# Second attention of a two-layer AdaLN block: one written-out turn per row tile, row and column parts of the array, mask added by VectorE

## The chip, the cores and the metric

One core of a Trainium2 chip. Times are device microseconds (us) of that core; a stage of the kernel is read from the profiled execution. Engines: TensorE (PE; PEld is its weight load), VectorE (DVE), ScalarE (ACT), GpSimd (POOL), SyncE (SP).

## The reference, cut to what matters

Two layers over x of 2048 rows by 512. Layer 0: AdaLN, windowed attention, AdaLN, a mixture of experts. Layer 1: AdaLN, the attention below, AdaLN, a feed-forward network with Hadamard transforms. What the change touches is the first half of layer 1 (all float32):

```
x   = x0 + sum over 8 slots of route_w[row, j] * y_moe[pos[row, j]]    # gathered expert rows
h   = layernorm(x) * (1 + scale) + shift
q   = rope(h @ Wq + bq)                    # 16 heads of 32
k,v = rope(h @ Wk + bk), h @ Wv + bv       # 4 key heads of 32, each serves 4 query heads
s   = q k^T / sqrt(32), masked: a row sees the 16 first keys (meta) and the last 128, never later ones
x   = x + gate * (softmax(s) v @ Wo + bo)
```

## The kernel before, in words

The work goes in 16 tiles of 128 rows. A tile's keys are 16 meta keys, its own 128 and those of the tile before: 272 columns (`KEYS1`). `prob` and `probT` are the probabilities of a head and their transposes.

`schedule` (L1367) makes turns; a turn works on six tiles at once, each one stage further: `g` gathers expert rows (POOL), `s` adds them up (DVE), `p` normalises and projects, `f` turns queries and keys, `m` does scores, softmax and values, `w` the output projection. The middle turns are a loop on the chip (`eng.Fori`, two tiles in a pass); each engine has its instructions in the order of its own `turn` function, and semaphores keep the engines apart.

Inside a turn all engines go by head, `n` from 0 to 15. For a head TensorE (L1574 on) adds the mask by a product of `ident_b` and `mask1` (L1588) and the scores (L1589) into bank `n % 4`; VectorE takes the negated maximum (L1704); ScalarE makes the exponentials from PSUM (L1544, L1545); TensorE transposes the two halves of 128 keys (L1594); ScalarE, and VectorE for every fourth head, copy them out (L1413); TensorE multiplies by the values, a matmul of 33 columns for each half (L1608, L1610), the 33rd being ones for the sum. A head's key tile `kT` is 128 partitions high and zero outside the head's own 32 rows, so a score product uses the whole array. Meta keys of 8 heads go together (L1596, L1613). `o_norm` divides by the sums, the result is transposed (L1647) and copied (L1750) before the product with `Wo` (L1659). The other steps hang between heads: transposes of h (L1639), queries (L1625) and keys (L1632), products with `Wq` (L1653) and `Wkv` (L1664); on VectorE the 8 expert additions (L1758), statistics (L1730 to L1734), normalisation (L1740), biases (L1764, L1777, L1780), residual (L1769); on POOL the power -1/2 (L1494), scale and shift (L1461, L1498), the output bias (L1504), the gathers (L1513), each behind a small `absorb` instruction (L1466), and the rotation `rotate` (L1461, L1488). Before the first turn POOL clears `kT`, `v` and `zeros_b` (L1454 on), and VectorE waits for all weights and multiplies `Wo` by the gate (L1672).

## Time and profile before

| | us |
|---|---|
| median of 3 runs | 2404.34 (2399.58 to 2405.88) |
| the profiled execution | 2407.0 |
| its span, first to last instruction | 2405.2 |
| second attention, first POOL instruction to last residual | 1215.5 to 1814.6 |

```profile
PE 2165.4 (90%) x11700; PEld 1492.4 (62%) x11702; DVE 1123.3 (47%) x2783; ACT 766.4 (32%) x1814; POOL 779.6 (32%) x1344
```

Busy time of each engine, share of the span, instructions. The matmul records overlap: a row's time for one matmul has its way through the array in it, so the rate is read from the distance of starts. A float32 matmul has two records. A busy TensorE is not one at its peak.

### The profile page before, as it was taken

The numbers are of one execution on the slowest core, as the hardware profiler recorded it, in microseconds if no ns is written. First come the engines' busy times: TensorE is split into PE (matmuls) and PEld (weight loads), VectorE is DVE, ScalarE is ACT, GpSimd is POOL, SyncE is SP. The second block draws the span as 40 slices with busy tenths as digits, with TensorE's granted clock in tenths as the row PEclk, the third lists the DMA queues.
The fourth block names the chain that finished last, engine by engine and source line by source line (L and its number), as shares of the span: only waits on it lengthen the run. The fifth ranks groups of instructions, "written<-read, shape, count | busy, mean of one in ns | idle before, by whom it ended". The sixth has DMA issues, their size and how long they took to land. (4 is left out here: it accounts for less than half of the span.)

```text
span 2405.2 us, 41150 instructions
## 1 busy us (share of the span) xinstructions
PE 2165.4 (90%) x11700; PEld 1492.4 (62%) x11702; DVE 1123.3 (47%) x2783; ACT 766.4 (32%) x1814; POOL 779.6 (32%) x1344
## 2 busy tenths in 40 slices
PE   4799877999999999999916999999994999999998
PEld 2676544555555555555504777777782887878787
DVE  2467575565552222222235676666543454343432
ACT  0233244222222222222202555444552332322322
POOL 0243302223333333333268766677312201101000
PEclk7899888999999999999957999999997999999999
DMA  7555542665565566656443222222001212222220
GB/s 243 183 203 199 218 125 84 195 201 176 183 203 183 191 214 203 203 189 221 136 150 89 72 56 57 72 71 72 2 1 53 70 62 79 62 73 67 72 68 27
DMA packets 122498, 302.21 MB, mean 126 GB/s; under 512 B 24864, under 2 KB 28576, under 8 KB 122272
## 3 DMA queue, kind: packets, MB, share of 16 engines
q1 hardware_dynamic: 73376, 179.04, 22.3%
q0 software_dynamic: 23040, 75.52, 11.1%
q10 hardware_dynamic: 25984, 46.38, 5.2%
q8 instruction: 58, 0.95, 0.2%
q14 instruction: 40, 0.33, 0.0%
HBM read 216.47 MB, written 83.36 MB: 125 GB/s over the span
## 5 line engine op out<-in xcount | busy, mean ns | idle before, releaser
L1167 PE MATMUL bank<-arena 128*128 x1272 | 446.4, 494 | 10.7 <-issue 9.2
L1167 PEld LDWEIGHTS bank<-arena 128*128 128x128 f32 x1272 | 229.8, 191 | 148.5 <-issue 17.9
L1184 PE MATMUL bank<-arena 96*128 x632 | 297.5, 593 | 0.0
L1288 DVE TENSOR_TENSOR arena<-bank,mod 128x512 f32<-128x512 f32 x158 | 109.3, 692 | 214.8 <-PE bank L1184 178.1
L1890 PE MATMUL bank<-x_hi,w_hi 128*128 128x512 f32 x512 | 200.8, 392 | 6.0 <-DVE x_lo L2023 6.0
L1890 PE MATMUL bank<-x_hi,w_lo 128*128 128x512 f32 x512 | 199.4, 389 | 0.0
L1890 PE MATMUL bank<-x_lo,w_hi 128*128 128x512 f32 x512 | 199.2, 389 | 0.0
L1283 DVE TENSOR_TENSOR arena<-arena,bank 128x192 f32<-128x192 f32 x159 | 56.3, 354 | 303.5 <-ACT arena L1205 303.1
L1200 ACT COPY arena<-bank 96x256 f32<-96x256 f32 x158 | 58.2, 368 | 423.2 <-issue 221.2
L1704 DVE TENSOR_REDUCE arena<-bank 128x1 f32<-128x272 f32 x256 | 112.1, 438 | 169.3 <-PE bank L1589 157.8
L1146 POOL DMA_INDIRECT arena<-h_moe,arena x160 | 158.5, 991 | 75.7 <-issue 73.0
L1145 POOL TENSOR_TENSOR arena<-neg_half 128x1 f32<-128x1 f32 x160 | 31.6, 197 | 461.4 <-PE bank L1176 461.1
L1589 PE MATMUL bank<-arena 128*128 128x272 f32 x512 | 160.5, 395 | 0.0
L1184 PEld LDWEIGHTS bank<-arena 96*128 96x128 f32 x632 | 107.3, 190 | 76.2 <-issue 76.2
L1544 ACT ACTIVATE arena<-bank,arena 128x16 f32<-128x16 f32 x256 | 70.6, 276 | 255.4 <-DVE arena L1704 225.3
L2103 DVE SCALAR_TENSOR_TENSOR ffn_arena<-bank,ffn_arena,mod 128x512 f32<-128x512 f32 x64 | 48.1, 751 | 221.3 <-PE bank L1890 174.3
L1513 POOL DMA_INDIRECT route_hot<-y_moe,arena x128 | 133.6, 1044 | 22.1 <-issue 12.6
L1545 ACT ACTIVATE arena<-bank,arena 128x256 f32<-128x256 f32 x256 | 119.9, 469 | 0.0
L1176 PEld LDWEIGHTS bank<-ident,arena 128*128 128x128 f32 x640 | 80.5, 142 | 60.2 <-issue 29.4
L1871 POOL TENSOR_TENSOR ffn_arena<-ffn_arena,neg_half 128x1 f32<-128x1 f32 x16 | 8.8, 550 | 328.7 <-DVE ffn_arena L2037 328.7
L1890 PEld LDWEIGHTS bank<-x_hi,w_hi 128*128 128x128 f32 x512 | 96.1, 188 | 28.7 <-issue 4.8
L1890 PEld LDWEIGHTS bank<-x_hi,w_lo 128*128 128x128 f32 x512 | 96.1, 188 | 20.2
(331 smaller groups left out, 4293.5 us busy)
## 6 DMA issues: line engine op xcount, KB each, us to landing
arena<-in_moe_up SPq DMA_DIRECT2D x64, 768.0 KB, 7.1
y_moe<-arena ACTq DMA_DIRECT2D x158, 256.0 KB, 2.7
y_moe<-mod SPq DMA_DIRECT2D x32, 1024.0 KB
ffn_arena<-in_ffn_up SPq DMA_DIRECT2D x64, 512.0 KB, 3.5
arena<-in_moe_down SPq DMA_DIRECT2D x64, 384.0 KB, 9.4
arena<-in_L_wmod SPq DMA_DIRECT2D x12, 1024.0 KB, 7.0
x_res<-in_L_attn_x SPq DMA_DIRECT2D x1, 4096.0 KB
h_moe<-arena SPq DMA_DIRECT2D x16, 256.0 KB, 6.7
```

The source lines that it names most:

```text
L1146: nc.gpsimd.indirect_dma_start(out=xg[:, b], out_offset=None, in_=h_moe, in_offset=bass.IndirectOffsetOnAxis(ap=st_tok[:, b], axis=0)).the ...
L1167: mm = nc.tensor.matmul(psum[2 + b][:, 0:2 * FI], xgT[:, b, k], up_ring[:, bass.ds((e % RING) * UPW + k * 2 * FI, 2 * FI)], start=(k == 0) ...
L1176: mm = nc.tensor.transpose(psum[b][:, k * P:(k + 1) * P], xg[:, b, k * P:(k + 1) * P], ident[:])
L1184: mm = nc.tensor.matmul(psum[6 + b][:], hiddenT[:, b, n], down_ring[:, bass.ds((e % RING) * DOWNW + n * C, C)], start=(n == 0), stop=(n == 1))
L1200: nc.scalar.copy(hiddenT[:, b], psum[4 + b][0:FH, 0:2 * P].rearrange("p (n q) -> p n q", n=2)).then_inc(hT_out, 1)
L1288: nc.vector.tensor_tensor(y[:, b], psum[6 + b][:], mod[:, 0, 5], ALU.mult).then_inc(y_out, 1)
L1513: nc.gpsimd.indirect_dma_start(out=yg[:, j], out_offset=None, in_=y_moe, in_offset=bass.IndirectOffsetOnAxis(ap=st_pos[:, j:j + 1], axis=0 ...
L1544: nc.scalar.activation(prob_meta[:, n // HM, n % HM], bank[:, 0:META], ACT.Exp, bias=bias)
L1545: nc.scalar.activation(prob[:, n % 4], bank[:, META:KEYS1], ACT.Exp, bias=bias).then_inc(exp_done, 1)
L1589: nc.tensor.matmul(bank, qT[:, b, n // HP], kT[:, n // HP, n % HP], start=False, stop=True).then_inc(s_mm, 1)
L1704: nc.vector.tensor_reduce(nmx[:, b, n:n + 1], psum[n % 4][:, 0:KEYS1], AX.X, ALU.max, negate=True).then_inc(mx_done, 1)
L1890: mm = nc.tensor.matmul(bank, x, y, start=(n == 0), stop=(n == len(passes) - 1))
```

## The change

The whole second attention is written anew. Turns are no longer a loop on the chip but written out, m from -4 to 17, with stages g (m+4), y (m+3, expert additions), p (m+2), f (m+1), s (m, scores and maxima), a (m-1, transposes and values) and w (m-2). Heads go in four groups `c` of four (`r`, by 32-row part of the array).

- Scores: q and k of head (c, r) lie in partitions 32r to 32r+31; four matmuls of 32 rows by 128 columns go to four banks. `kT` is 4 x 272 columns instead of 16 x 272. No mask product.
- VectorE adds the mask, negates, stores and takes the minimum in one `tensor_tensor_reduce` a head, then one subtraction of 4 x 16 meta scores a group. ScalarE exponentiates in place in SBUF: 16 of 256 columns, and all meta scores of a tile in one.
- Probabilities are transposed four heads at a time into banks 4 and 5, and copied by ScalarE alone, 512 columns each.
- Values are taken transposed: output partitions 32c to 32c+31 are the 32 values of group c, columns are 4 x 128 queries; the sums come from the same products with `ones_f`. Both at the end of TensorE's turn. `oT` is so had without a transpose: VectorE takes the reciprocal of 512 sums and multiplies.
- The order on VectorE: normalisation of p, division of w, then four `maxima`, with the expert additions (3, 2, 3), biases, residual and kx between them, and the statistics of y last.
- POOL gathers in parts of 3, 2 and 3 with one `absorb` each; the copies of values and of positions are gone; the first gather comes before the clearing of `kT`. `Wo` is loaded in four DMAs (its rows in another order) and multiplied by the gate in turn m = -1.
- `h` lies in `down_scale`, `oT`, `osum`, `hT`, `rot`, `prob_meta` in the free `mod[:, 0]`.

```diff
-DVE_B, POOL_B = 14, 40
+            VRING, GROUPS = 5, 6
+            def schedule(turn):
+                tile = lambda t: t if 0 <= t < NT else None
+                for m in range(-4, NT + 2):
+                    turn(g=tile(m + 4), y=tile(m + 3), p=tile(m + 2), f=tile(m + 1), s=tile(m), a=tile(m - 1), w=tile(m - 2))
@@ gpsimd
+                def gather(t, js):
+                    if t:
+                        pool.wait_ge(y_sum, TOPK * (t - 1) + js[-1] + 1)
+                    absorb()
+                    for j in js: ...                      # indirect DMA of yg[:, j]
+                def turn(g, y, p, f, s, a, w):
+                    if p is not None:
+                        pool.wait_ge(stats, p + 1)
+                        ...                               # pow -> rstd; wait xhat; h * mod + mod -> h_done
+                    if w is not None: ...                 # x_res += bo
+                    if g: gather(g, range(0, 3))
+                    if p is not None: ...                 # wait q_rows; rotate 16 query heads -> roped_q
+                    if g: gather(g, range(3, 5))
+                    if p is not None: ...                 # wait kv_rows; rotate 4 key heads -> roped
+                    if g: gather(g, range(5, TOPK))
@@ tensor
+                def scores(t, c):
+                    ...
+                    pe.wait_ge(mx_done, NHEAD * t + HP * c)
+                    for r in range(HP):
+                        q = slice(HD * r, HD * r + HD)
+                        nc.tensor.matmul(psum[r][:, 0:KEYS1], qT[q, t % 2, c], kT[q, c], start=True, stop=True).then_inc(s_mm, 1)
+                def turn_probs(t, c):
+                    pe.wait_ge(exp_done, NHEAD * t + HP * c + HP)
+                    if c == 0 and t: pe.wait_ge(o_out, t)
+                    pe.wait_ge(pT_out, copies_before(t, c))
+                    ...                                   # 8 transposes into psum[4], psum[5]
+                # turn: scores(s,0) | h transposes(p) | qT(f) | turn_probs(a,0) | Wq(p) | scores(s,1) | turn_probs(a,1)
+                #       | Wkv(p) | scores(s,2) | turn_probs(a,2) | Wo(w) | turn_probs(a,3) | scores(s,3) | meta transposes(a)
+                #       | kT(f), waits x_out(w) | values(a)
+                        for bank, local, meta in ((b_o, v ..., v_meta ...), (b_sum, ones_f, meta_sum ...)):
+                            for k in chunks(a):
+                                for c in range(NKV1):
+                                    nc.tensor.matmul(bank[HD * c:HD * c + HD], local(k, c), probT[:, k, c].rearrange("p r n -> p (r n)"),
+                                                     start=(k == 0), stop=False)
+                            for r in range(HP):
+                                for c in range(NKV1):
+                                    mm = nc.tensor.matmul(bank[HD * c:HD * c + HD, r * P:(r + 1) * P], meta(r, c), metaT[:, c // 2],
+                                                          start=False, stop=(r == HP - 1))
@@ vector
+                def maxima(t, c):
+                    ...
+                    for r in range(HP):
+                        n = HP * c + r
+                        dve.wait_ge(s_mm, NHEAD * t + n + 1)
+                        nc.vector.tensor_tensor_reduce(slot(t, c)[:, r], psum[r][:, 0:KEYS1], mask1[:, kind], -1.0, 3e38, ALU.add, ALU.min,
+                                                       accum_out=nmx[:, t % 2, n:n + 1]).then_inc(mx_done, 1)
+                    dve.wait_ge(mx_done, NHEAD * t + HP * c + HP)
+                    ...                                   # prob_meta = nmx - slot, 4 x 16 columns -> meta_sub
+                def turn(g, y, p, f, s, a, w):
+                    if p is not None: ...                 # wait rstd; normalise -> xhat
+                    if w is not None: ...                 # wait o_mm; reciprocal(osum, b_sum); oT = b_o * osum -> o_out
+                    if f == 0: weights_ready(); meta_values()
+                    # maxima(s,0) | kx(f) | experts(y) 0-2 | q bias(p) | maxima(s,1) | experts 3-4 | k, v bias(p)
+                    # | maxima(s,2) | experts 5-7 | residual(w) -> x_out | maxima(s,3) | statistics(y)
```

The lines with `|` and the comments stand for the calls of the new text in their order; ScalarE's new turn is: copy hT(p), copy qT(f), then for c = 0 to 3 two copies of turned probabilities (a) and four exponentials (s), before the last of which it also copies the meta probabilities and kT(f); at the end the meta exponential.

## Rows read from the trace of the kernel before

**Rows 1.** Busy time by stretch: stretch, length, busy of PE, PEld, DVE, ACT, POOL, clock, DMA.
```profile
1383.00:1715.00 332.00, 316.28 (x1928) 241.29 (x1927) 226.02 (x482) 166.95 (x511) 218.76 (x324) 1.00 0.21 60
```
**Rows 2.** Who waited for whom, 1215 to 1840 us: total, times, longest.
```profile
DVE arena L1704 <- PE bank L1589: 157.8, 133, 4.3
```
**Rows 3.** Instructions in order of time, TensorE, one head: start, us, records.
```profile
1488.69 0.28 PE L1588 MATMUL bank<-mask,ident_b 128*128 128x272 bf16 x1
1488.81 0.62 PE L1589 MATMUL bank<-arena 128*128 128x272 f32 x2
1489.27 0.38 PE L1594 MATMUL bank<-ident,arena 128*128 128x128 f32 x2
1489.49 0.31 PE L1608 MATMUL bank<-arena 128*128 128x33 f32 x2
```
**Rows 4.** The same view: the query projection of two tiles nine turns apart.
```profile
1404.84 3.60 PE L1653 MATMUL bank<-arena 128*128 128x512 f32 x8
...
1703.05 3.60 PE L1653 MATMUL bank<-arena 128*128 128x512 f32 x8
```
**Rows 5.** The same view: matmuls of 32 by 64 tiles in the first attention, two windows.
```profile
106.61 0.37 PE L523 MATMUL bank<-arena 32*64 32x64 f32 x16
106.61 0.91 PE L523 MATMUL bank<-arena 32*64 32x64 f32 x64
```
**Rows 6.** In order of time on VectorE; the L1017 row is that line's instruction view.
```profile
1502.79 0.43 DVE L1704 TENSOR_REDUCE arena<-bank 128x1 f32<-128x272 f32 x1
1503.14 0.74 DVE L1758 SCALAR_TENSOR_TENSOR x_res<-route_hot,route_w,x_res 128x512 f32 x1
...
1233.95 6.96 DVE L1758 SCALAR_TENSOR_TENSOR x_res<-route_hot,route_w,x_res 128x512 f32<-128x512 f32 x8
...
1525.86 0.69 DVE L1730 BATCH_NORM_STATS2 arena<-x_res 128x6 f32 x1
...
1526.81 0.15 DVE L1734 TENSOR_SCALAR arena<-arena 128x1 f32<-128x1 f32 x1
...
L1017 DVE DVE_READ_ACCUMULATOR arena<-arena,iota_col x1: 82/82/82, 336.7 to 336.7; 128x1 f32 x1
...
L701 DVE RECIPROCAL arena<-bank 128x8 f32<-128x8 f32 x32 | 4.4, 180 | 2.1 <-PE bank L596 2.1
```
**Rows 7.** In order of time on POOL, one turn: start, us, idle before.
```profile
1545.24 0.97 POOL L1513 DMA_INDIRECT route_hot<-y_moe,arena  x1 [0.15 <-issue]
1546.23 2.98 POOL L1461 TENSOR_TENSOR arena<-arena 128x256 f32<-128x256 f32 x3
1549.29 1.27 POOL L1488 TENSOR_TENSOR arena<-arena 128x512 f32<-128x512 f32 x1
...
1555.14 1.19 POOL L1461 TENSOR_TENSOR arena<-arena 128x64 f32<-128x64 f32 x3 [1.88 <-DVE arena L1780]
1556.41 0.46 POOL L1488 TENSOR_TENSOR arena<-arena 128x128 f32<-128x128 f32 x1
1560.25 0.58 POOL L1494 TENSOR_TENSOR arena<-arena,neg_half 128x1 f32<-128x1 f32 x1 [3.38 <-DVE arena L1734]
1561.93 1.71 POOL L1461 TENSOR_TENSOR arena<-arena,mod 128x512 f32<-128x512 f32 x1 [1.10 <-DVE arena L1740]
1563.72 1.26 POOL L1498 TENSOR_TENSOR arena<-arena,mod 128x512 f32<-128x512 f32 x1
1565.31 1.73 POOL L1504 TENSOR_TENSOR x_res<-x_res,arena 128x512 f32 x1
```
**Rows 8.** In order of time: start of the stage, and its last instruction.
```profile
1234.98 0.65 POOL L1466 TENSOR_TENSOR arena<-neg_half 128x1 f32<-128x1 f32 x1 [3.65 <-DMA route_hot<-y_moe,arena]
1252.61 1.11 PE L1639 MATMUL bank<-ident,arena 128*128 128x128 f32 x4 [48.35 <-POOL arena L1498]
1254.49 5.87 PE L1653 MATMUL bank<-arena 128*128 128x512 f32 x8 [0.77 <-ACT arena L1566]
1813.91 0.69 DVE L1769 TENSOR_TENSOR x_res<-bank,x_res 128x512 f32<-128x512 f32 x1 [5.44 <-PE bank L1659]
```
**Rows 9.** POOL in order of time while VectorE adds experts.
```profile
1254.17 1.58 POOL L1513 DMA_INDIRECT route_hot<-y_moe,arena  x1 [0.16 <-POOL arena L1466]
```

More of the change, by code:

```diff
@@ L1368, in adaln_two_layers @@
-            N_DMA = 8
-            def schedule(eng, turn, steps=None, per=0):
-                stages = (4, 3, 2, 1, 0, -1)
-                def tile(t):
-                    return (t, t % 2, t // 2) if 0 <= t < NT else None
-                for t in range(-4, 4):
-                    turn(*[tile(t + n) for n in stages])
-                turns = (NT - 8) // 2
-                with eng.Fori(0, turns) as i:
-                    if steps:
-                        steps.loop(i, per)
-                    for t in (4, 5):
-                        turn(*[(i * 2 + (t + n), (t + n) % 2, i + (t + n) // 2) for n in stages])
-                if steps:
-                    steps.end(turns)
-                for t in range(NT - 4, NT + 1):
-                    turn(*[tile(t + n) for n in stages])
@@ L1439, in _ @@
                 tables = a["rope"].rearrange("(t p) k d -> t p k d", p=P)
-                def turn(g, s, p, f, m, w):
-                    if s is not None:
-                        t, b, half = s
-                        wait_tile(sp, roped, 1, shift(t, -2))
-                        one = tables[t] if isinstance(t, int) else tables[bass.ds(t, 1)].rearrange("o p k d -> (o p) k d")
-                        sp.dma_start(rope[:, b], one).then_inc(rope_in[b], 16)
-                schedule(sp, turn)
+                def turn(g, y, p, f, s, a, w):
+                    if y is not None:
+                        if y >= 2:
+                            sp.wait_ge(roped, y - 1)
+                        sp.dma_start(rope[:, y % 2], tables[y]).then_inc(rope_in[y % 2], 16)
+                schedule(turn)
                 for b in range(2):
@@ L1466, in absorb, with rotate @@
                     st.did(nc.gpsimd.tensor_tensor(spare[:, 0:1], neg_half[:], neg_half[:], ALU.add))
[L1468 to L1476 removed]
+                def rotate(t, rows, at, n):
+                    b = t % 2
                     x = qk[:, b, rows]
@@ L1530, in _ @@
+                    if g:
+                        gather(g, range(3, 5))
+                    if p is not None:
+                        pool.wait_ge(kv_rows, p + 1)
+                        rotate(p, slice(NHEAD, NQK), 2, NKV1).then_inc(roped, 1)
+                    if g:
+                        gather(g, range(5, TOPK))
+                schedule(turn)
             @block.scalar
@@ L1569, in _, with exps, copy_pT @@
-                schedule(act, turn)
+                def exps(t, c):
+                    for r in range(HP):
+                        n = HP * c + r
+                        act.wait_ge(mx_done, NHEAD * t + n + 1)
+                        some = slot(t, c)[:, r, META:KEYS1]
+                        nc.scalar.activation(some, some, ACT.Exp, bias=nmx[:, t % 2, n:n + 1], scale=-1.0).then_inc(exp_done, 1)
+                def copy_pT(t, c):
+                    if t and c == 0:
+                        act.wait_ge(o_mm, 2 * NKV1 * t)
+                    for n, k in enumerate(chunks(t)):
+                        act.wait_ge(pT_mm, copies_before(t, c) + n + 1)
+                        copy(probT[:, k, c].rearrange("p r n -> p (r n)"), psum[4 + k][:]).then_inc(pT_out, 1)
@@ L1668, in _ @@
+                schedule(turn)
             @block.vector
@@ new lines, in meta_values @@
+                def meta_values():
+                    head = meta_head.rearrange("p (c r) -> p r c", c=2).unsqueeze(3).to_broadcast([P, HP, 2, HD])
+                    st.did(nc.vector.tensor_copy(meta_sum[:], head))
+                    dve.wait_ge(meta_mm, 1)
+                    for n in range(2):
+                        rows = b_sum[:, n * 2 * HD:(n + 1) * 2 * HD].rearrange("p (c d) -> p c d", c=2)
+                        st.did(nc.vector.tensor_tensor(v_meta[:, n], rows.unsqueeze(1).to_broadcast([P, HP, 2, HD]), head, ALU.mult))
+                    st.settle()
+                    dve.sem_inc(v_meta_done, 1)
```

610 lines of the change are left out of this document (276 added, 334 removed).

## The prediction

> **What bounds the kernel now.** I read the busy time by stretch first, then who waited for whom, then the engines in order of time. In the steady stretch of the second attention TensorE is busy 316 of 332 us at the full clock (1.00, the 2.4 GHz level), VectorE 226, POOL 219, ScalarE 167 [rows 1]. VectorE's longest wait is for the score matmul, 157.8 us in 133 times [rows 2]. So TensorE sets the pace. One head shows on what it spends it: a mask product (0.12 us from start to start), a score product (0.46), two transposes (0.22), then the four value records, which end where the next head begins, 1.16 us after the last one as the sum of the steps; a score product of 272 columns has all 128 array rows for 32 that matter [rows 3]. Nine turns lie between the two query projections shown: 298.2 / 9 = 33.1 us a tile [rows 4]. Sixteen heads are 18.6 of it, the rest mostly the projections: four products of 512 columns are 3.60 us [rows 4], 0.85 each.
>
> **What the change takes from TensorE.** Whether the array's parts really run beside each other is the first question. The first attention does it with 32 by 64 parts: 64 records of 64 columns last 0.91 us together [rows 5]; with some 0.22 for the last one's way through the array they start 11 ns apart. At 0.85 us for 512 columns in two records a record of 64 takes 53 ns, so about 5 run at once; four row parts alone would give 13 ns apart, so column halves overlap as well. Sixteen records within 0.37 us [rows 5] say the same. I take four row parts and four column parts as concurrent. Then, per turn:
> - Scores: four groups of 272 columns, 0.46 plus weight load, 0.57 each: 2.3 us.
> - Transposes: 32 at 0.11 [rows 3] and 2 meta, 3.7; 12 of h, q, k, 1.5.
> - Projections 3.6 + 3.6 + 1.8 = 9.0.
> - Values: for each of two banks two rounds of 512 columns (1.7) and four meta rounds of 128 (0.85), 2.75 with the rounds' edges: 5.5. Nothing in the trace runs four column parts with four streams. Bounds: all serial, 8 x 0.85 + 16 x 0.25 a bank, 22 us for both; two at a time 11; four at a time 5.1. I take 5.5, nearest to rows 5.
>
> That sums to 22 us for some 31, with nothing on the other engines in it. So the next question is what is late in its place.
>
> The Trainium skill (TensorE: Matmul & The Clock Gate, Measured speedup vs the span model) gives 2.38 times for three column parts. By it my 5.1 would be 6.5, an estimate, a turn would be half of 1.4 longer and the total some 14 us more, 2293; rows 5, with 5 of 8, lie in the same manner below the ideal. The Trainium skill (TensorEngine Tiling, Key Properties) also says that a change of the tiling mode drains the array; no row here prices one, and ten switches a turn fall mostly into TensorE's slack in the walk below.
>
> **What it adds elsewhere, step by step.** VectorE's prices from start to start: maximum 0.35 [rows 6]; expert addition 0.87 in a run of eight, each waiting for the last [rows 6]; 512 columns from PSUM 0.6 (the residual's 0.69 [rows 8] less the 0.08 by which the maximum's 0.43 outlasts its 0.35); the normalisation 0.55, bounded by 1.10 from the end of the power to the start of the scaling [rows 7]. The new operation isn't in the trace. From below it costs the plain maximum, 0.35; from above a maximum and an addition one after the other, 0.70. An accumulator is read out by an instruction of 82 ns [rows 6]; I take 0.46. A group of four with the wait and the subtraction is 2.2. The reciprocal of 8 columns takes 180 ns [rows 6], no dearer than other small operations; for 512 I take 0.75, bounds 0.6 and 1.2. Statistics: 1525.86 to 1526.96, 1.1 [rows 6]. Copies of 512 by ScalarE fill 0.77 with the hand-overs [rows 8]; its turn is some 13 us and never last.
>
> POOL's prices [rows 7]: power 0.58, scale and shift with gap 3.05, output bias 1.73, rotation of queries 2.98 + 0.08 + 1.27 = 4.35, of keys 1.75, a gather 1.0, an absorb with its wait 0.3.
>
> Now one steady turn, zero at the start of the normalisation, which heads VectorE's queue and waits for POOL's power:
> - h is ready at 0.55 + 0.07 + 3.05 = 3.7. TensorE: four transposes to 4.35, four of q, eight of probabilities, projection 5.6 to 9.2.
> - VectorE divides w once the values of the last turn are there (V): 1.4; maxima 2.2; kx 0.35; three experts 2.6: done at V + 6.6. It then waits for 9.25. Queued behind that wait are all its later steps.
> - q bias 0.6, maxima 2.2, two experts 1.75, k and v biases 0.6, maxima 2.2, three experts 2.6: 19.2. Residual to 19.9, maxima to 22.0, statistics to 23.1, power and hand-over to 23.8. On TensorE meanwhile: scores and probabilities to 10.5, Wkv to 12.4, third scores and probabilities to 13.75, Wo to 17.3, probabilities, and the last scores at 18.1, none late for VectorE. So VectorE's ring is 23.8.
> - TensorE's end: key transposes after the residual, 19.95 to 20.45, values to 26.1. So V = 26.1 - T.
> - POOL cannot begin the gathers before y_sum counts three: V + 6.6. From there 3.3 + 4.35 + 2.3 + 1.75 + 3.3 = 15.0, then the power 0.65: T = V + 22.25. With V = 26.1 - T, T = 24.2.
>
> So a turn is about 24.2 us, set by a ring through POOL and the values, VectorE's own being 0.4 shorter: 8.9 less than before. The mechanism of the title, normalisation first, only starts h early; the price is that VectorE stands at the head of its turn until the power is there.
>
> **Start and end.** Before, h of tile 0 reaches TensorE at 1252.61, as VectorE waits for all weights and POOL clears 16 x 272 columns [rows 8]. After, eight gathers go out from 1215.5, land 3.65 us after the last [rows 8], experts and statistics of tile 0 end about 1229; but POOL's second set of gathers lasts until 1234.2, and its power comes behind them: normalisation at 1234.9, h at 1238.5. Turns -2 and -1 have cold projections (5.87 for 3.6, 1.2 GHz) [rows 8]; -2 takes 24.9 (q bias at 1247.1, rotation, gathers, keys, gathers, power), -1 takes 26.5 (plus gate and meta values). Turn 0 starts its normalisation at 1286.2. The weights (landed at about 1231) and the four Wo DMAs are hidden: they are wanted at 1240. Twelve turns of 24.2, then one without gathers, 23.8: 1600.4. Turn 13 to the end of its values: 25.4; turns 14, 15, 16 without normalisation run on the order scores, maxima, scores with TensorE, 19.1, 18.6, 18.2; the last division, Wo and residual 6.5: 1688.2. Before: 1813.91 [rows 8]. The gain is 125.7 us. The profiled execution took 2407.0, so 2281.3; the median shown is 2.7 below it: 2279. What else moves (no loop, semaphores, `h` in another tile) I cost at nothing; the first attention is written out as well and shows no gap for it.
>
> Bounds on the turn: with 0.35 for the new operation POOL's ring still gives 23.6 (2272); with 0.70 VectorE's ring is 23.8 + 12 x 0.24 = 26.7 (2311). Own range of the forecast: 2255 to 2312.
>
> **Rivals.**
> - *POOL is slowed by the expert additions.* Eight additions now lie beside POOL's gathers and rotations. For: a gather took 1.58 beside them [rows 9] and 0.97 otherwise [rows 7]. Against: only the ones that start under an addition pay. If all eight pay, POOL's part is 19.9 and T = (26.1 + 22.25 + 4.9) / 2 = 26.6: 12 x 2.4 = 29 us, 2308. The Trainium skill (SBUF, State Buffer; two separate sides) says that a VectorE operation with two SBUF inputs and a GpSimd one lock each other out; by that rule, rows 9 agree.
> - *Only two column parts run at once.* Values 11: the ring runs from the division through maxima, experts, projections and residual (17.2), the key transposes 0.5 and the values: 29. 12 x 4.8 + 4 x 5.5 = 80: 2359. For: rows 5 show two column halves, no more.
> - *Column parts do not overlap when each spans all 128 rows (slower than before).* Values 22, ring 17.2 + 0.5 + 22 + 0.2 = 39.9: 12 x 15.7 + 4 x 16.6 = 254 us more, 2533. It decides from values of about 14 us on, where the gain of 126 is eaten. For: the records of rows 5 could get their overlap beyond four by pipelining alone. Against: 11 ns is below 13.
> - *Waits are shorter than I walked.* If POOL keeps ahead and the maxima are at the low price, T nears 22.5: 12 x 1.7 = 20, 2259, a little less at the ends: down to 2240.
>
> **How the numbers follow.** Forecast 0.58, POOL slowed 0.16, two parts 0.09, serial 0.07, shorter waits 0.10. All but the serial one are faster: 0.92, as something unseen could also cost a gain, the rest 0.01 within 0.3% (7 us, about what a measurement here can tell) and 0.07 slower. The range takes the first two, the low one and half of the two-part case: 2238 to 2345.
>
> **What would show it right or wrong.** Score matmuls of one group starting nanoseconds apart; the values of a turn in 5 to 7 us (11 or 22 for the rivals); projections 24 to 25 us apart; VectorE's longest waits at the normalisation for POOL's power and at the q bias; POOL busy over 80% of the stretch; TensorE near 85% at clock 1.00; first h transposes near 1238, last residual near 1688. I am wrong if TensorE stays the engine all wait for, if its clock falls in its new gaps, or if a turn is under 22 or over 28 us.

## The result, and the profile after

2369.4 us (median of 4 runs, 2367.6 to 2371.8) beside 2405.1 before (2399.6 to 2409.9) on the same chip: 0.9854 of the time, 95% interval 0.9834 to 0.9874. Faster, clear of the noise though by less than 2%: 36 us where 125 were forecast, and outside the range (2238 to 2345).

The profiled execution took 2370.2 us, its span 2366.9. The second attention's last residual starts at 1774.42 instead of 1813.91 [rows 8]. The page's first part, then the busy time of the steady stretch (it answers to rows 1: length, PE, PEld, DVE, ACT, POOL, clock, DMA):

```profile
PE 2059.5 (87%) x11764; PEld 1340.5 (57%) x11766; DVE 1122.9 (47%) x2920; ACT 708.0 (30%) x1455; POOL 726.6 (31%) x1164
```
```profile
1383.00:1640.00 257.00, 218.41 (x1727) 126.19 (x1731) 200.72 (x512) 117.33 (x260) 170.38 (x201) 0.95 0.27 74
```

No engine is full: PE 85%, DVE 78%, POOL 66%, and the granted clock is 0.95 where rows 1 had 1.00. Something goes round between engines. Who waited for whom, 1350 to 1650 us (total, times, longest; four of its rows):

```profile
POOL arena L1422 <- DVE x_res L1701: 65.7, 10, 7.4
DVE down_scale L1720 <- POOL arena L1457: 24.9, 10, 4.4
DVE mod L1725 <- PE bank L1643: 19.7, 11, 2.7
PE bank L1556 <- issue: 18.3, 8, 2.6
```

POOL waits 6.6 us a turn for the third expert addition, VectorE for POOL's power (L1457) and for the value products (L1643). The last row is TensorE before it turns the probabilities; the profile names no releaser for it, but the code has it wait for the division there. One turn in order of time, cut to the steps that matter (start, us, idle before):

```profile
1518.75 0.63 PE L1630 MATMUL bank<-ident,arena 128*128 128x128 f32 x4 [2.10 <-DVE x_res L1767]
1519.31 3.20 PE L1639 MATMUL bank<-arena 128*32 128x512 f32 x16
1522.26 1.53 PE L1643 MATMUL bank<-arena 128*32 128x128 f32 x32
1523.27 0.55 DVE L1720 TENSOR_SCALAR down_scale<-x_res,arena 128x512 f32<-128x512 f32 x1 [1.94 <-POOL arena L1457]
1523.61 1.90 PE L1639 MATMUL bank<-arena 128*32 128x512 f32 x16
1525.33 1.06 PE L1643 MATMUL bank<-arena 128*32 128x128 f32 x32
1526.32 0.74 PE L1546 MATMUL bank<-arena 32*128 32x272 f32 x8
1526.53 3.36 DVE L1725 RECIPROCAL mod<-bank 128x512 f32<-128x512 f32 x1 [2.72 <-PE bank L1643]
1529.92 0.69 DVE L1727 TENSOR_TENSOR mod<-bank,mod 128x512 f32<-128x512 f32 x1
1530.71 1.94 PE L1556 MATMUL bank<-ident,arena 128*128 128x128 f32 x8 [2.64 <-issue]
1532.45 4.11 PE L1590 MATMUL bank<-arena,mod 128*128 128x512 f32 x8
1532.57 2.46 DVE L1701 SCALAR_TENSOR_TENSOR x_res<-route_hot,route_w,x_res 128x512 f32<-128x512 f32 x3
1535.10 0.19 POOL L1422 TENSOR_TENSOR arena<-neg_half 128x1 f32<-128x1 f32 x1 [7.35 <-DVE x_res L1701]
1552.67 0.58 POOL L1457 TENSOR_TENSOR arena<-arena,neg_half 128x1 f32<-128x1 f32 x1
1553.29 0.55 DVE L1720 TENSOR_SCALAR down_scale<-x_res,arena 128x512 f32<-128x512 f32 x1 [1.94 <-POOL arena L1457]
```

Follow it down. Values end (1526.4), VectorE divides (3.36 + 0.69), only then the turned probabilities (L1556) may overwrite banks 4 and 5; the query projection (L1590) is queued behind them. After maxima and three additions POOL may gather (1535.10) and is done 17.6 us later (1552.67). The next normalisation is 30.0 us after this one. The turn shown is one of the long ones: the residuals (L1767) of the steady turns are 27.5 to 30.1 apart, 29.2 in the mean of nine, and from the normalisation of turn 0 to that of turn 12 a turn takes 28.7 us, where 24.2 was forecast.

Two things hold in every steady turn. The value products, from the first record of L1639 to the last of L1643, take 7.1 us here (1519.31 to 1526.39) and 6.9 to 7.2 in the others; in the five turns without gathers they take 5.4:

```profile
1690.87 1.92 PE L1639 MATMUL bank<-arena 128*32 128x512 f32 x16
1692.58 1.08 PE L1643 MATMUL bank<-arena 128*32 128x128 f32 x32
1693.45 1.93 PE L1639 MATMUL bank<-arena 128*32 128x512 f32 x16
1695.17 1.08 PE L1643 MATMUL bank<-arena 128*32 128x128 f32 x32
```

And VectorE and POOL hold each other up. The subtraction of 64 columns behind the second maxima lasts until POOL's two rotation products are done; behind the third it takes 0.23:

```profile
1508.55 2.17 DVE L1694 TENSOR_TENSOR mod<-arena 128x64 f32<-128x64 f32 x1
1508.97 1.66 POOL L1417 TENSOR_TENSOR mod<-arena 128x256 f32<-128x256 f32 x2
1515.06 0.23 DVE L1694 TENSOR_TENSOR mod<-arena 128x64 f32<-128x64 f32 x1
```

### The profile page after: what moved, and what is told of

Read it like the earlier page. It is cut to its first block and busy times, and to the rows that moved or that the text cites. A ratio compares the mean times of both kernels' runs of the same rounds, so it can differ in the third digit from the quotient of the medians.

```text
span 2366.9 us, 39347 instructions
## 1 busy us (share of the span) xinstructions
PE 2059.5 (87%) x11764; PEld 1340.5 (57%) x11766; DVE 1122.9 (47%) x2920; ACT 708.0 (30%) x1455; POOL 726.6 (31%) x1164
## 5 line engine op out<-in xcount | busy, mean ns | idle before, releaser
L1445 POOL DMA_INDIRECT route_hot<-y_moe,pos_u x128 | 125.5, 981 | 32.1 <-issue 27.9
L1701 DVE SCALAR_TENSOR_TENSOR x_res<-route_hot,route_w,x_res 128x512 f32<-128x512 f32 x128 | 115.4, 902 | 25.5 <-DMA route_hot<-y_moe,pos_u 17.7
L1492 ACT ACTIVATE arena<-arena 128x256 f32<-128x256 f32 x256 | 109.2, 502 | 18.7 <-DVE arena L1690 18.6
L1175 PEld LDWEIGHTS bank<-ident,arena 128*128 128x128 f32 x640 | 80.2, 141 | 58.9 <-issue 28.7
L1556 PE MATMUL bank<-ident,arena 128*128 128x128 f32 x496 | 78.4, 309 | 34.3 <-issue 31.9
L1881 PEld LDWEIGHTS bank<-x_lo,w_hi 128*128 128x128 f32 x512 | 96.2, 188 | 19.4
```

The lines of the kernel that those rows point to most:

```text
L1175: mm = nc.tensor.transpose(psum[b][:, k * P:(k + 1) * P], xg[:, b, k * P:(k + 1) * P], ident[:])
L1445: nc.gpsimd.indirect_dma_start(out=yg[:, j], out_offset=None, in_=y_moe, in_offset=bass.IndirectOffsetOnAxis(ap=pos_u[:, t, j:j + 1], axis ...
L1492: nc.scalar.activation(some, some, ACT.Exp, bias=nmx[:, t % 2, n:n + 1], scale=-1.0).then_inc(exp_done, 1)
L1556: mm = nc.tensor.transpose(psum[4 + k][:, r * P:(r + 1) * P], slot(t, c)[:, r, at:at + P], ident[:])
L1701: nc.vector.scalar_tensor_tensor(x_res[:, t], yg[:, j], route_w[:, t, j:j + 1], x_res[:, t], ALU.mult, ALU.add).then_inc(y_sum, 1)
L1881: mm = nc.tensor.matmul(bank, x, y, start=(n == 0), stop=(n == len(passes) - 1))
```

## The experiments

Times are medians. A ratio, with its 95% interval, is to the kernel before, run beside it. The changed kernel, 2369.4, is what the differences in us refer to. Unless said, each edit is made to the changed kernel.

**1. The price of the reciprocal.** The copy leaves the division out of the result.
```diff
-                        st.did(nc.vector.reciprocal(osum, b_sum[:]))
+                        st.did(nc.vector.tensor_copy(osum, b_sum[:]))
```


> The changed kernel with VectorE's reciprocal of 512 sums replaced by a copy of them, so the division is left out of the result. Theory A (the reciprocal, 3.36 us where 0.75 was reckoned, lies on the ring values -> division -> maxima -> residual -> key transposes -> values and nothing else is late right behind it): each of some 14 turns shrinks by about 2.7 us of 29.2, total 2369 - 38 = 2331 (2322 to 2340). Rival B (POOL's gathers and power are the ring and the reciprocal only fills a wait): under 1 us a turn, above 2355. Rival C (what is lost is TensorE's clock in the gap before the division): the clock goes to 1.00 in the steady stretch and the gain is over 50 us, under 2320.


2316.7 us, 0.9649 [0.9633, 0.9666]: 53 us under the changed kernel, in rival C's band and not in theory A's. The trace says where. The twelve turns from 0 on are 26.0 us long for 28.7, which is 2.7 us a turn, just the price of the reciprocal; that is 32 us, and theory A holds there (the clock is 0.96, not C's 1.00). From the normalisation of turn 13 to the last residual it takes 85.0 us for 107.5, which is 22.5 less where five reciprocals are 13, and the granted clock of that stretch is 1.00 for 0.87: the low clock is a part of the loss at the end.

**2. Only the sums hold the reciprocal.** The products with ones go first and count a semaphore of their own; VectorE divides beside the value products.
```diff
-  for bank, ... in ((b_o, v...), (b_sum, ones_f...)):
+  for bank, ..., done in ((b_sum, ones_f..., sum_mm), (b_o, v..., o_mm)):
-                        dve.wait_ge(o_mm, 2 * NKV1 * (w + 1))
+                        dve.wait_ge(sum_mm, NKV1 * (w + 1))     # and o_mm before the multiplication
```


> The changed kernel with the sums' products ahead of the values' products and their own semaphore, so that the reciprocal runs beside the 2.7 us of value products. No work is taken away. Theory A: 2.5 us of the reciprocal hide in the turns that wait for the values today (two of three), 0.5 in the others: some 26 us, 2343 (2332 to 2352). Rival B (POOL sets the turn): above 2360.


2329.0, 0.9688 [0.9672, 0.9704], 40 under the changed kernel and 3 below the expected band. The twelve turns give 19 (27.1 us each), the end 22 (85.5 us, clock 1.00), which the expectation had not priced.

**3. The first three expert additions ahead of the division**, to let POOL start early.
```diff
                         nc.vector.tensor_scalar(h, x_res[:, p], ...).then_inc(xhat, 1)
+                    if y is not None:
+                        for j in range(0, 3):
+                            add_expert(y, j)                    # taken from behind kx
```


> The changed kernel with the first three expert additions moved from behind the first maxima to right behind the normalisation, into VectorE's wait for the values. Theory A: 2.4 us leave the ring behind the division, and POOL gets its leave to gather some 8 us sooner: about 2.4 us a turn, 2336 (2325 to 2348). Theory B (POOL's chain of gathers and rotations from the third addition on sets the turn): POOL's part now starts 8 us earlier, turn limited by VectorE's own sum of 24 to 25 us: 4 us a turn or more, under 2320. If neither the division ring nor POOL is late, no change.


2390.2, 0.9958 [0.9942, 0.9975]: 21 us slower, against both theories. Its trace in order of time:
```profile
1504.48 4.09 DVE L1701 SCALAR_TENSOR_TENSOR x_res<-route_hot,route_w,x_res 128x512 f32<-128x512 f32 x3
1504.64 1.70 POOL L1417 TENSOR_TENSOR down_scale<-down_scale,mod 128x512 f32<-128x512 f32 x1 [0.66 <-DVE down_scale L1720]
1508.49 3.35 DVE L1728 RECIPROCAL mod<-bank 128x512 f32<-128x512 f32 x1
1512.66 1.94 PE L1556 MATMUL bank<-ident,arena 128*128 128x128 f32 x8 [3.49 <-issue]
1514.39 5.12 PE L1590 MATMUL bank<-arena,mod 128*128 128x512 f32 x8
1519.55 0.69 DVE L1746 TENSOR_TENSOR arena<-bank,arena 128x512 f32<-128x512 f32 x1 [4.96 <-PE bank L1590]
```
The three additions last 4.09 us beside POOL's scaling, 2.46 where they stood before. The value products end at 1505.44, but the division starts 3 us behind that; TensorE stands 3.49 us, runs the projection at 5.12 for 3.60, and VectorE pays at the query bias. POOL gathers early, as meant, but then stands 6.84 us until the query rows are there. This showed the edge that my walk lacked: division, turned probabilities, query projection, query bias, in TensorE's queue order.

**4. Normalisation behind the division.**
```diff
-   normalisation of p; division of w
+   division of w; normalisation of p
```


> The changed kernel with the normalisation put behind the division on VectorE, undoing the title's last clause. If h is early enough only thanks to that order: normalisation starts some 7 us later in a turn, the query projection waits for h and starts some 4 us later, the turn grows by 3 to 4 us: 2369 + 50 = 2419 (2400 to 2430). If the rings through the values or through POOL alone set the turn, within 10 us of 2369.


2398.1, 0.9987 [0.9977, 0.9998], 2 below the band of the first theory; granted clock 0.87 in the stretch. The normalisation ahead of the division, which the prediction and this expectation call the title's though the title does not name it, is worth 29 us to this kernel. Without it the rest of the change is worth 4.

**5. The query projection ahead of the turned probabilities.**
```diff
+ Wq(p)
  if a is not None: turn_probs(a, 0)
- Wq(p)
```


> The changed kernel with the query projection ahead of the first eight probability transposes in TensorE's order. Today those transposes wait for the division and the projection stands behind them (1532.45 where h was turned at 1528.1). Theory A (the division holds the projection, and with it VectorE's q bias): the 1.6 us by which VectorE waits for the projection in two of three turns go, 0.2 in the others: 14 turns by 1.2, 2352 (2343 to 2360). Rival (VectorE's own sum behind the division sets the turn, the q bias would be caught up): no change within 5 us.


2353.9, 0.9789 [0.9773, 0.9805]: 15.5 us, 15 of them in the twelve turns. The edge of 3 is real.

**6. Two more products of 512 columns in TensorE's wait for the division** (their bank is written over).
```diff
+ for _ in range(2):
+     nc.tensor.matmul(bb[:], hT[:, 0], wq[:, 0], start=True, stop=True)
  turn_probs(a, 0)
```


> The changed kernel with two more products of 512 columns (1.7 us, overwritten by the projection) in TensorE's wait for the division. If the clock's fall in that gap costs: the transposes take 1.1 for 1.9 and the projection 3.6 for 4.1, the granted clock of the steady stretch is 0.99 or more for 0.95, and 10 of 14 turns gain 1.3 us: 2356 (2350 to 2362). If the slow stretch is only caught in VectorE's slack, the time stays within 4 us of 2369 though the clock rises. If the filler is too short to hold the clock, both stay.


2360.0, 0.9817 [0.9801, 0.9834]: more work, 9 us less. The query projection takes 3.60 in every steady turn, where it takes 3.60 to 5.29 without, so what stands behind the gap is back at the full clock. The stretch's mean clock, 0.96 for 0.95, is not the 0.99 that was expected: TensorE still waits for the residual (9.7 us in 10 times) and runs slowly behind that wait. The low clock behind the first gap costs about 9 us, a side cause.

**7. Key transposes behind the values**, and ScalarE's copy of them behind the meta exponential.
```diff
- kT(f), waits x_out(w) | values(a)
+ values(a) | kT(f), waits x_out(w)
```


> The changed kernel with the key transposes behind the values instead of ahead of them, so the values no longer wait for the residual (2.1 us idle a turn); ScalarE's copy of the keys moves behind its meta exponential. Theory A: values end 2.6 us sooner, 2.5 of the wait before the division goes in two of three turns: 1.7 us by 14, 2345 (2335 to 2353). Rival (POOL's gathers set the turn): within 5 us of 2369.


2348.5, 0.9759 [0.9742, 0.9776], 21 us, as expected: the wait of L1630 for the residual (2.10 us in the turn shown) leaves the way to the values.

**8. Edits 2, 5 and 7 together.**


> Sums first, query projection ahead and key transposes last, together. With the ring through values and division open at three places, VectorE's own work is left: 23.4 us busy a turn plus the wait for POOL's power (2) and small ones, 25.5 for 29.2: 14 x 3.7 = 52, 2317 (2305 to 2325). If POOL's chain behind the third expert addition sets the turn (9.1 from power to third addition, 17.5 to the end of the gathers): 27.3, 2342.


2336.4, 0.9717 [0.9701, 0.9733]: 33 us where the parts sum to 77, and slower than edit 2 alone (2329.0). Waits of this kernel, 1350 to 1650 us:
```profile
POOL arena L1422 <- DVE x_res L1701: 45.9, 10, 4.9
DVE down_scale L1720 <- POOL arena L1457: 34.3, 11, 4.4
PEld bank L1569 <- POOL down_scale L1461: 20.9, 11, 3.2
```
Each of the three shortens the way through TensorE. What is left, by the turn of 27.2 us and the second theory of the expectation, is POOL's ring alone (9 puts it to the test): power, normalisation, division, maxima, kx, three additions, POOL's 17.6 us, power.

**9. Edit 2, with the first three additions directly behind the division** (ahead of the first maxima and kx).
```diff
   nc.vector.tensor_tensor(oT..., b_o[:], osum, ALU.mult).then_inc(o_out, 1)
+  for j in range(0, 3): add_expert(y, j)
   ...
   maxima(s, 0)
   nc.vector.tensor_copy(kx[:], ...)
-  for j in range(0, 3): add_expert(y, j)
```


> The sums' products first (as in e2_sums_first, 2329 us), and the first three expert additions directly behind the division's multiplication, ahead of the first maxima and of the copy kx. Theory POOL ring: once the division no longer waits for the value products, the ring is power, normalisation, division, first maxima, kx, three expert additions, then POOL's 17.5 us of gathers and rotations to the next power. The edit takes the maxima (1.7 us) and kx (about 1.3 us) out of it, so some 3 us of a turn: 2329 less 12 x 3 = 2293 us (2283 to 2312). Rival, VectorE's own work or TensorE is the bound in e2: the order changes nothing, 2323 to 2335 us. A rival on the other side: the first scores' maxima late by three additions (2.5 to 4 us) hold the exponentials and the turned probabilities, over 2340 us.


2309.0, 0.9601 [0.9584, 0.9618], 60 us under the changed kernel and 20 under edit 2. Busy time of its steady stretch, and three rows on the ring:
```profile
1383.00:1640.00 257.00, 243.19 (x2041) 143.71 (x2034) 227.05 (x582) 135.30 (x297) 192.77 (x222) 1.00 0.28 77
```
```profile
1457.15 0.59 POOL L1457 TENSOR_TENSOR arena<-arena,neg_half 128x1 f32<-128x1 f32 x1
1457.78 0.55 DVE L1720 TENSOR_SCALAR down_scale<-x_res,arena 128x512 f32<-128x512 f32 x1 [1.95 <-POOL arena L1457]
1458.24 3.35 DVE L1725 RECIPROCAL mod<-bank 128x512 f32<-128x512 f32 x1
```
From the power to the division's start is 1.1 us, the reciprocal and the multiplication 4.0, the three additions 2.5, and from there POOL needs 17.8 to its next power: 25.4. In these rows none of them waits for anything outside the ring. The residuals are 25.36 to 25.38 us apart in nine turns on end. The clock is back at 1.00, PE 95% busy. What I had filed under clock and TensorE's queue went with the ring.

**10. Edits 2, 5, 7, with the three additions ahead of the division.**


> Sums' products first, query projection ahead of the turned probabilities, key transposes last (as g3_three, 2336 us), and the first three expert additions behind the normalisation, ahead of the division. Theory POOL ring: division, maxima and kx (4.0 + 1.7 + 1.3 us) all leave the ring, and VectorE's own work is the next bound, some 2 us shorter than g3's turn of 27.2: about 2310 us (2295 to 2322). Rival, taken from e3_experts_early: the additions run beside POOL's scale and shift at 1.36 us each, the division begins 3 to 4 us later, TensorE waits for it behind the query projection and its clock falls: 2345 us or more.


2318.9, 0.9652 [0.9627, 0.9677]. With the query projection ahead, the order of 3 no longer hurts (turn 25.65). It isn't the best, but not for the additions beside POOL's scaling: with the additions behind the division (16) it is 2320.0. What both have and kernel 9 hasn't are edits 5 and 7.

**11. All chunks of one column part, then the next part** (the two loops of the value products exchanged).
```diff
-  for k in chunks(a):
-      for c in range(NKV1):
+  for c in range(NKV1):
+      for k in chunks(a):
```


> The value and sum products in another order: all keys' chunks of one column part, then the next part, where the changed kernel takes the four parts in turn for each chunk. The results are the same. If four products of different column parts run together only because they follow each other in the queue, then the 16 products 128x512 of a bank take 16 times about 0.45 us (a product of the query projection), 7.2 us where they took 1.90, 10.6 us more in a turn of two banks, and the kernel takes 2369 + 12 x 10 = 2490 us (2450 to 2530). If the products of one part are as quick (the parts never ran together, or are found anyway), it stays within 10 us of 2369.


2369.4, 0.9853 [0.9837, 0.987]; 16 records last 1.94 us (1.92 in the changed kernel at the same place). No difference, 121 us from what was expected. Either the parts do not run together, or two products in a row to one part don't break it.

**12. Half of the value products sent to part 0.** The other parts' share of the second chunk of keys is left out of the result.
```diff
-  nc.tensor.matmul(bank[HD * c:HD * c + HD], local(k, c), ...
+  nc.tensor.matmul(bank[0:HD] if k else bank[HD * c:HD * c + HD], local(k, c), ...
```


> The changed kernel, where the value and sum products of the second chunk of keys all go to column part 0 (half of the 512-column products; the other parts miss that chunk's share). If products of different column parts run together and those of one part one after the other, a bank's 16 records take 0.9 us for the first chunk and 4 x 0.9 = 3.6 us for the second, 4.5 in place of 1.90, 5.2 us more in a turn of two banks, and 2369 + 12 x 5 = 2430 us (2405 to 2445). If a product with 32 columns of weights is simply quick, it stays within 10 us of 2369.


2423.4, 1.0086 [1.0065, 1.0107], 54 us more. On TensorE, one bank:
```profile
1506.61 0.61 PE L1639 MATMUL bank<-arena 128*32 128x512 f32 x3
1506.69 0.27 PE L1643 MATMUL bank<-arena 128*32 128x128 f32 x1
1506.80 4.03 PE L1639 MATMUL bank<-arena 128*32 128x512 f32 x12
```
The bank's 512-column products take 4.2 us (1506.61 to 1510.83) for 1.90. So different parts do run together and one part's products one after the other. With 11, it follows that there the pair of one part overlaps with the next part's.

**13. The weight load waits for tile 0's gathers.**
```diff
+                sp.wait_ge(y_in[TOPK - 1], 16)
                 sp.dma_start(wq[:], ...)
```


> The changed kernel, where the DMA queue of the second attention's weights waits until the eight gathers of tile 0 have landed. Theory: the start was 12.6 us later than reckoned because the expert rows came in 1.3 to 2.9 us apart beside the weight load; without it the first normalisation of the ring is 5 to 12 us earlier, and the end too: 2360 us (2355 to 2366). Rival: POOL's issue at 1.25 us a gather sets the start alone, and the weights then come late for the first query projection: 2366 us or more.


2372.7, 0.9871 [0.9853, 0.9889]; a miss, and the rival's band. Counted from the first gather of its own run, the first normalisation comes after 23.1 us for 26.3 (the time at which the stage begins moves by up to 10 us from run to run, so points of two runs are compared this way). But the first query projection then waits 10.16 us for the weights:
```profile
1237.35 0.55 DVE L1721 TENSOR_SCALAR down_scale<-x_res,arena 128x512 f32<-128x512 f32 x1 [7.99 <-POOL arena L1458]
1252.67 5.09 PE L1591 MATMUL bank<-arena,mod 128*128 128x512 f32 x8 [10.16 <-DMA arena<-in_meta_head]
```
Here the expert rows came early at the cost of the weights.

**14. Kernel 9 with the copy for the reciprocal** (the division is left out).


> h1_experts_mid with a copy of 128x512 for the reciprocal (the sums are multiplied in place of their reciprocals, so the division is left out): about 0.7 us in place of 3.35, which is the price that the prediction took. POOL ring 25.4 - 2.65 = 22.7 us, TensorE's 24.0 is the next bound: 2309 less 12 x 1.3 = 2293 us (2284 to 2300). Rival, the whole 2.65 comes off: 2277 us.


2305.9, 0.9595 [0.9574, 0.9616]: 3 us where experiment 1 gave 53, and 6 above the expected band. The turn is 25.21. VectorE's multiplication now waits 1.86 us for the value products, and TensorE stands only for the residual, 1.31 us a turn:
```profile
1456.99 0.69 DVE L1728 TENSOR_TENSOR mod<-bank,mod 128x512 f32<-128x512 f32 x1 [1.86 <-PE bank L1643]
1474.67 0.63 PE L1630 MATMUL bank<-ident,arena 128*128 128x128 f32 x4 [1.31 <-DVE x_res L1768]
```
So what holds this turn is no full engine but a ring through two: multiplication to residual 17.5 us, key transposes 0.7, values 6.9 (1475.22 to 1482.07), and the multiplication again. At the values' 5.4 us of the turns without gathers this ring would be 23.7, an estimate, below the 24.2 of the forecast. In kernels 9 and 14 each full pass of value products with gathers in its turn loses 1.4 to 1.5 us against the last one (one of twenty only 1.0), from about its 43rd record of 96 on, and none of the five without gathers loses anything. No run here shows what stops TensorE there.

**15. Kernel 9 with the reciprocal on ScalarE**, as the exponential of the negative logarithm.
```diff
+  nc.scalar.activation(osum, b_sum[:], ACT.Ln).then_inc(ln_done, 1)        # head of ScalarE's turn, waits sum_mm
+  act.wait_ge(ln_done, w + 1)
+  nc.scalar.activation(osum, osum, ACT.Exp, scale=-1.0).then_inc(os_done, 1)
-  st.did(nc.vector.reciprocal(osum, b_sum[:]))
```


> h1_experts_mid (2309 us, a turn of 25.37 us), with the reciprocal taken from VectorE: ACT takes the logarithm of the sums and the exponential of its negative (2 x about 0.6 us at the head of its turn, once the sums' products are done), and VectorE's multiplication follows the normalisation directly. Theory POOL ring: 0.55 + 3.35 + 0.69 + 2.8 (three additions) + 17.5 (POOL) + 0.6 (power) is h1's 25.4; without the 3.35 it is 22.1, and the next bound is TensorE, busy for 0.95 of h1's turn, 24.0: 2309 less 12 x 1.3 = 2293 us (2280 to 2299). Rival, nothing stands behind the reciprocal as the next bound (VectorE's own work, 22.4 less 3.4): 2309 less 12 x 3.3 = 2269 us. Rival on the other side: ACT, whose exponentials of the first scores now stand behind these two, or changes of its function table at every turn (two a turn), makes it slower: over 2312 us.


2301.3 (2299.6 to 2305.3), 0.9577 [0.9559, 0.9595]: the fastest found, 68 us under the changed kernel and 8 under kernel 9. The turn is 25.2 as in 14, so it is 8 us above what I expected and 2 above the band. Of the 8 us, each counted within its own run, about 1 comes in the twelve turns, 4 in the last five, which go by the way through the division, and 3 in the start.

**16. Edits 2, 5, 7 with the additions behind the division.**


> g3_three (sums first, query projection ahead of the turned probabilities, key transposes last, 2336 us) with the first three expert additions directly behind the division. If the ring is POOL's, as in h1, the other two reorderings have nothing left to give: 2309 us within 6. If TensorE's order still mattered behind it, up to 12 us less: 2297. Rival on the other side: the key transposes, late, hold the next scores: 2318 us or more.


2320.0, 0.9657 [0.9634, 0.968]. It is 11 us above kernel 9, in the band of the expectation's last rival. The turn is POOL's 25.38 again, so the other two edits have nothing to give in it; two turns are 26.3 and 26.5, and the last turns are longer (the residuals 25.84 and 23.26 apart where kernel 9 had 24.15 and 21.79). That the late key transposes hold the scores is likely, as TensorE waits 8.7 us in 12 times ahead of scores and in kernel 9 has no such wait, but not shown to be all of it.

**17. Kernel 15 with the key transposes behind the values.**


> h4_recip_on_act (2301 us, turn 25.2) with the key transposes behind the value products. Theory, TensorE is the bound: its one wait of the turn (1.3 to 1.6 us for the residual) goes, the turn is 24.0, the prediction's 24.2 nearly, and 2301 - 12 x 1.2 = 2287 us (2280 to 2293). Rival: the late key transposes hold the next first scores behind ACT's copy (h2_three_mid lost in this way), and the wait only moves: 2298 us or more.


2348.4, 0.9765 [0.975, 0.978]; a clear miss, the rival's side. With the query projection ahead too it is 2346.9, 0.9757 [0.9742, 0.9772], within the 4 us of this one that were expected. ScalarE and VectorE in order of time:
```profile
1460.34 0.59 ACT L1541 COPY arena<-bank 128x512 f32<-128x512 f32 x1 [4.11 <-PE bank L1652]
1460.94 1.28 ACT L1506 ACT_TABLE_LOAD   x1
1462.23 0.60 ACT L1506 ACTIVATE mod<-bank 128x512 f32<-128x512 f32 x1
1462.85 1.28 ACT L1508 ACT_TABLE_LOAD   x1
1464.15 0.63 ACT L1508 ACTIVATE mod<-mod 128x512 f32<-128x512 f32 x1
1464.86 0.69 DVE L1733 TENSOR_TENSOR mod<-bank,mod 128x512 f32<-128x512 f32 x1 [5.81 <-ACT mod L1508]
```
The logarithm is queued behind the copy of the keys, which now comes last on TensorE; with two table loads the multiplication is 5.8 us late. In kernel 15 the loads are there too (L1506 at 1475.82, L1508 at 1478.22), but the first lies in ScalarE's wait for the sums, and the multiplication waits 2.5 us. So this run does not test whether TensorE alone would hold the 25.2 us; the ring of 14 says that it doesn't.

## Why the prediction was wrong, step by step

**The step that failed is "for 512 I take 0.75, bounds 0.6 and 1.2" for the reciprocal.** It takes 3.36 us in each of 16, 6.6 ns a column. It was priced from the 8-column reciprocal of rows 6 (180 ns), a duration in which the fixed part hides the part that grows with the columns; the upper bound of 1.2 had no row under it. The trace of the kernel before had two more groups of reciprocals to hold against it (busy time, then mean ns of one, behind the first bar):

```profile
L1692 DVE RECIPROCAL arena<-bank 128x8 f32<-128x8 f32 x32 | 6.3, 196 | 3.1 <-PE bank L1613 3.1
L665 DVE RECIPROCAL arena<-arena 128x2 f32<-128x2 f32 x8 | 1.3, 167 | 0.3
```

The second reads SBUF and not PSUM. Six columns more cost 13 ns (180 for 167) or 29 ns (196 for 167). By that growth alone 512 columns would be some 1.3 to 2.6 us, an estimate from these rows: still too low, but both above my upper bound. With a copy of 0.69 us in its place, about the price that I had reckoned, the kernel takes 2316.7 (1): inside the range and 38 above the forecast. So this term holds 53 of the missing 90 us in the order of the changed kernel.

**The second step is an edge that the walk left out.** In TensorE's queue the query projection stands behind the turned probabilities, and these wait for the division. With the reckoned 0.75 the edge would have been hidden; with 3.36 it is on the ring, and 5 takes 15.5 us away with it alone.

**The ring was right in form.** I wrote V = 26.1 - T and T = V + 22.25, so T = 24.2 (V is the end of the values behind a normalisation, T the turn). In the turn shown, values end 3.1 us after the normalisation and 3.0 after the next:
- From the values' end to the third addition: 8.7 us, not 6.6 (the division 4.1 for 1.4, the maxima's group 1.7 for 2.2).
- POOL from there to the power: 17.6, not 15.0. A gather comes every 1.25 us (0.95 and 0.30 of issue) for my 1.0; rotation and absorbs take the rest. So T = V + 26.9.
- Normalisation to the end of the values: 33.0, not 26.1. The query bias is 4.1 us late: the query projection starts at 9.2 for 5.6, by the edge above, and takes 4.11 for 3.60 at a lower clock. From there to the end of the key transposes it is 1.5 more, in the stretch where VectorE and POOL hold each other up. The values take 6.9 us (1549.34 to 1556.26) where the walk has 5.6 (20.45 to 26.1; its own price of 5.5 would end them at 25.95).
- (26.9 + 33.0) / 2 = 29.95, measured 30.0.

**Where the 86 us are** by which the last residual is later than forecast (1774.42 for 1688.2):
- Start, 12.6: turn 0's normalisation at 1298.76 for 1286.2. h of tile 0 is there at 1245.29, reckoned 1238.5, as its expert rows land 1.2 to 2.9 us apart beside the weights and POOL's gathers come at 1.25.
- Twelve turns, 53.7: 28.7 us each for 24.2. The thirteenth is 24.0 for 23.8.
- End, 19.7: from the normalisation of turn 13 to the last residual 107.5 for 87.8. Turns 14 to 16, from values' end to values' end, take 22.1, 22.5 and 23.9 for 19.1, 18.6 and 18.2. Each has the reciprocal in line, and the stretch's clock is 0.87. With the sums first (2) it is 85.5, at clock 1.00.

Experiments 9, 14 and 15 give the rest of the proof: in another order, and with the reciprocal in its place, the operations of the changed kernel run at 25.4 us a turn, and there the dear reciprocal costs only 0.16 us, because a second ring stands right behind POOL's (14).

**Right:** TensorE set the pace before and does so no more. Four row parts run together: a group of scores takes 0.74 us, 0.67 from start to start, for 0.57. Four column parts too: 5.4 us for both banks in the turns without gathers, for 5.5; but 6.9 to 7.2 in the others, which I had not foreseen. The serial rival and the one with two parts fall, and 12 shows the cause. The new operation costs 0.36 from start to start, at the low end of 0.35 to 0.70. VectorE's longest wait is for the power, as said (24.9 us); the query bias, which I named second, is third (12.5), behind the value products (19.7). POOL is busy 66% of the stretch, not over 80.

**Rivals:** "POOL is slowed by the expert additions" is real: the last step of the query rotation takes 1.60 for 1.27 [rows 7]. But VectorE is slowed more. In the steady stretch an addition takes 0.75 alone and 1.09 to 1.58 in 15 of 72, a subtraction 0.23 or 1.08 to 2.31: together some 2.4 us a turn on VectorE, an estimate from these durations. How much of it reaches the ring was not tested; the 1.5 us above are its bound in that turn. The Trainium skill (SBUF, State Buffer, in its section SBUF: two separate sides) says that a VectorE operation with two SBUF inputs and a GpSimd operation that reads SBUF share a pair of ports, and the one blocks the other for its whole length; the subtraction of 2.17 us, which ends with POOL's rotation products, agrees. I had it as a rival for POOL alone and gave VectorE's side no price beside the 0.87 of an addition. Shorter waits: no. By my own test, "if its clock falls in its new gaps, or if a turn is under 22 or over 28 us", I was wrong on both.

## What to carry to other kernels

Price an operation by its column count from a row of like size, and where there is none, leave the range as wide as the fixed and the growing part together allow; two small sizes, here 2 and 8 columns, at least show that there is a growing part. In a ring through several engines write every queue order edge, above all what stands behind a bank's reader on TensorE. Before making a dear operation cheaper, move what the other engines wait for: two reorderings, the sums first on TensorE (40 us) and three additions ahead of the maxima on VectorE (20 more), gave more than leaving the reciprocal out did (53), while three reorderings of TensorE, each good alone, did not add up.

## What the runs showed of the hardware

- A reciprocal of 128 x 512 from PSUM on VectorE: 3.36 us; a copy of the same: 0.69 (1).
- An expert addition (two SBUF inputs, 128 x 512) takes 0.75 us alone. Beside POOL's scaling (3) two of three took 1.56 and 1.57, and the scaling went from 1.28 to 1.70.
- Products of 512 columns to one column part run one after the other (4.2 us a bank with half of them in one part), to four parts together (1.92), and two in a row to the same part cost nothing (1.94).
- The 96 value records of a turn take 5.4 us in turns without gathers and 6.8 to 6.9 in nearly all with gathers, though the granted clock is 1.00 in the stretch with gathers and 0.96 in the one without (9, 14). The cause is open.
- Alternating logarithm and exponential came with two table loads of 1.28 us in every turn (15, 17).
- More TensorE work in a gap made the kernel 9 us faster (6).
